# Products of the register rows over the 16 value columns of a head, and the experts' bias products on four row groups

## Chip, core and metric

The kernel is one program on one core of a Trainium2 chip. The metric is the device time of one execution in microseconds (us), lower is better; times of a kernel are medians over several executions. All data are float32. In the trace every float32 matmul of the program appears as two pairs of instructions, a weight load (PEld, LDWEIGHTS, the stationary operand) and a matmul (PE, MATMUL, the moving operand), so that four products of the program are 8 rows' worth of instructions. A float32 transpose appears as one such pair.

## What is computed

Four layers run over `x` of 8 tiles (sequences) x 512 tokens x 256 channels. Each does `x = x + s(xn) * silu(f(xn))` with `xn` the layer norm of `x`. Two places matter here. The gate branch of layer 1 is a mixture of 8 experts over all tokens:

```python
logits = xt @ Wr + br
gates = entmax_bisect(logits)                       # (tokens, 8), 25 bisection steps
gates = where(gates > 1e-9, gates, 0)
h = relu(einsum('td,edf->etf', xt, W1) + b1[:, None, :])    # F = 1024
y = einsum('etf,efd->etd', h, W2) + b2[:, None, :]
out = einsum('etd,te->td', y, gates)                # so b2 enters as gates @ b2
```

The gate branch of layer 3 is attention in which the first 5 tokens of a sequence are register rows (16 heads of 16 channels). An ordinary token sees only keys of its own set (and the registers); a register row takes the mean of two attentions, one over each set:

```python
x_pos, x_neg = masked_attn(pos), masked_attn(~pos)
reg_out = (x_pos[:, :REG] + x_neg[:, :REG]) * 0.5
tok_out = where(pos, x_pos[:, REG:], x_neg[:, REG:])
```

## The kernel before

Every layer is one block in which TensorE, VectorE (DVE), ScalarE (ACT), GpSimd (POOL) and SyncE (SP, it issues the transfers) each follow an order of instructions written out by hand; semaphores join them. PSUM banks are handed round by the classes `Jobs` (layer 1) and `Flow` (layer 3): `open` makes TensorE wait until the bank's last user has emptied it, `fill` marks the last matmul into it, `wait_filled` and `empty` are the reader's side.

**Layer 1** (function `layer1`) goes through the 8 tiles one after the other. For a tile TensorE does, in this order: the convolution's inputs `xb` (L1152) and `z` (L1157); `expert_in(0)` (L1112: for each of 8 blocks f of 128 hidden units, two products of 512 columns into one of two banks `hid`, which ACT empties with a relu, L1236); `expert_in(1)` without its last block; then, once DVE has the gates, the transposes `gt` of the gates (L1104, four tiles of 128 tokens x 8 experts into one bank of 8 x 512); the last block of `expert_in(1)`; the four bias products `b20` to `b23` (L1169: 8 experts x 128 tokens against `b2`, 8 x 256, each into a bank of its own); `expert_out(0)` (L1122: for each of 4 token tiles j, 8 products of 256 columns into one of two banks `exp_out`); `expert_in(2)`; the running sums `cum` of the state space part; and so on through expert 7. All matmuls of L1169 stand on partitions 0 to 7, so on the first of the array's four groups of 32 rows.

DVE, meanwhile: copy `gt` out (L1407), copy the four `b2` banks to `moe` (L1410), wait for its own last copy, then the convolution (L1420, L1422), four taps of 5 instructions; after tap k it adds the product of expert 0 and token tile k (`expert_sum`, L1403), for which it waits if TensorE has not filled the bank. The last tap sets `conv_ready`. ACT does the relus of experts 0 and 1, waits for `conv_ready`, and then mixes silus of the convolution (L1257, two at a time, then L1260, L1261) with relus of expert 2: two silus, relu 0, two silus, relu 1, two short silus, relu 2, and the rest. `expert_in(2)` needs bank 0 of `hid` back after its second block (relu 0), bank 1 after the third (relu 1) and bank 0 after the fourth (relu 2).

The gates of the next tile are found by DVE during expert 7 and the next tile's first products; those of the first tile have nothing before them, and TensorE stands waiting for them once.

**Layer 3's** second block (`layer3_sets`) runs 16 steps per tile. In a step TensorE does four score products and four transposed score products (L386, L393, each of 32 rows x 512 columns on one of the four row groups), the value products of the step before (L408), and a share of the work around the attention, in `last_tile`, `this_tile` and `next_tile`. The values `v_ones` hold 32 columns per head: 16 of the value, a one and zeros. In step 15 `this_tile` multiplies the transposed weights of the register rows (`reg_prob_t`, 128 x 128 for each of 4 key tiles) with all 512 columns of `v_ones` (L2872, bank `rv`). DVE waits for that bank, takes 16 of each head's 32 columns, times the inverse sum and a mask, to `reg_y` (L3093), and goes on with the next layer norm and row maxima. TensorE later sums `reg_y` over the heads (L2839).

Of the kernel before, what the change touches and what calls it, by code (L numbers as in the profile page):

```python
# [19 lines left out]
P = 128  # L20
# [940 lines left out]
def layer1(nc, b2_dram, w1_dram, w2_dram, x_all, cst, ahead, norms):  # L961
    (WZ, WX, WBC, WS, WO, CW, CB, SB, ALOG, DROW, NW, B1), width = spans(*L1_SIZES)
    with ExitStack() as ctx:
        a = Alloc(nc, ctx, "l1")
        w, b2 = ahead.w, a.sb("b2", [E, C])
        w1, w2 = a.sb("w1", [P, 2, CT, F]), a.sb("w2", [P, 2, HF, C])
        norm = ahead.norm
        xn, xn_t = norm.xn, a.sb("xn_t", [P, CT, T])
# [14 lines left out]
        half, tau_lo, width_, tau = a.sb("half", [P, TJ, E]), a.sb("tau_lo", [P, TJ]), a.sb("width_", [P, TJ]), a.sb("tau", [P, TJ])  # L983
        over, part, mass, mass_lo, step = (a.sb("over", [P, TJ, E]), a.sb("part", [P, TJ, E]), a.sb("mass", [P, TJ]),
                                           a.sb("mass_lo", [P, TJ]), a.sb("step", [P, TJ]))
        gates, gates_t = a.sb("gates", [P, TJ, E]), a.sb("gates_t", [E, T])
        hidden, moe = a.sb("hidden", [P, 2, HF, T]), a.sb("moe", [P, TJ, C])
        s = y[:, :, 0:C]

# [49 lines left out]
        @block.sync  # L1039
        def _(sp):  # L1040
            def load(e):
                sp.dma_start(w1[:, e % 2], w1_dram[e]).then_inc(w1_loaded[e % 2], 16)
                sp.dma_start(w2[:, e % 2], w2_dram[e]).then_inc(w2_loaded[e % 2], 16)

            def spread_cums(j):
                sp.dma_start(mix[:, j % 2].rearrange("p h l -> p (h l)"),
                             cum_dram[j].rearrange("h l -> (h l)").partition_broadcast(P)).then_inc(cum_loaded[j], 16)

            def stream(b, n, jobs):
                for e in range(n):  # L1050
                    nxt = (e + 2) % E
                    hid.wait_filled(sp, b, (e, HF - 1))
                    sp.dma_start(w1[:, e % 2], w1_dram[nxt]).then_inc(w1_loaded[e % 2], 16)
                    if e == 1:
                        jobs.wait_emptied(sp, b, "cum")
                        sp.dma_start(cum_dram.rearrange("j h l -> (j h) l"), cum_rows[:, :]).then_inc(cum_written, 16)
                        sp.wait_ge(cum_written, 16 * (b + 1))
                        spread_cums(0)
                        spread_cums(1)
                    if 2 <= e < TJ:  # L1060
                        jobs.wait_filled(sp, b, f"yd{e - 2}")
                        spread_cums(e)
                    exp_out.wait_filled(sp, b, (e, TJ - 1))
                    sp.dma_start(w2[:, e % 2], w2_dram[nxt]).then_inc(w2_loaded[e % 2], 16)

            sp.dma_start(b2[:, :], b2_dram).then_inc(b2_loaded, 16)
            load(0)
            load(1)
            with sp.Fori(0, B - 1) as b:
                stream(b, E, ring)  # L1070
            stream(B - 1, E - 2, last_ring)

        @block.tensor
        def _(pe):
# [23 lines left out]
            def sequence(b, is_last):  # L1098
# [60 lines left out]
                expert_in(0)  # L1159
                expert_in(1, range(HF - 1))  # L1160
                pe.wait_ge(gates_ready, b + 1)
                tiles_t("gt", lambda j: gates[:, j, :], E, 0)
                expert_in(1, [HF - 1])
                jobs.wait_emptied(pe, b, "gt")
                if b == 0:
                    pe.wait_ge(b2_loaded, 16)
                for j in range(TJ):
                    bank = jobs.open(pe, b, f"b2{j}")
                    jobs.fill(nc.tensor.matmul(bank[:, 0:C], gates_t[:, j * P:(j + 1) * P], b2[:, :], start=True, stop=True), f"b2{j}")  # L1169
                for e in range(E):  # L1170
                    if e >= 1:
                        if e + 1 < E:
# [151 lines left out]
        def _(dve):  # L1324
# [2 lines left out]
                uses.start_empty(dve)  # L1327
            dve.wait_ge(ahead.w_loaded, 16)
            V.memset(xbc[:, :, 0:TAPS - 1], 0.0)
            for f in range(FT):  # L1330
                V.tensor_scalar(wo[:, f, :], wo[:, f, :], w[:, NW][:, f:f + 1], None, ALU.mult).then_inc(prepared, 1)
            dve.wait_ge(act_prepared, 1)
# [46 lines left out]
            def sequence(b, is_last):  # L1379
# [24 lines left out]
                                                         ALU.mult, ALU.add), (e, j))  # L1404

                bank = jobs.wait_filled(dve, b, "gt")
                jobs.empty(V.tensor_copy(gates_t[:, :], bank[0:E, :]), "gt")  # L1407
                for j in range(TJ):
                    bank = jobs.wait_filled(dve, b, f"b2{j}")
                    jobs.empty(V.tensor_copy(moe[:, j, :], bank[:, 0:C]), f"b2{j}")  # L1410
# [1337 lines left out]
def layer3_sets(nc, w_dram, l3c, x_all, s_all, meanvar, rstd, set_q, set_k, cst, out_dram):  # L2748
# [6 lines left out]
    with ExitStack() as ctx:  # L2755
# [40 lines left out]
        def _(pe):  # L2796
# [60 lines left out]
            def this_tile(b, i):  # L2857
                if i == 4:
                    pe.wait_ge(reg_ready, b + 1)
                    att.wait_moved(pe, b, 3)  # L2860
                    bank = flow.open(pe, "score", ("rs", b))
                    for g in range(G):
                        ins = nc.tensor.matmul(bank[g * SLOT:(g + 1) * SLOT, :], reg_blocks[:, g, :], att.k_t[:, g, :], start=True, stop=True)  # L2863
                    flow.fill(ins, ("rs", b))
                elif i == 7:
                    flow.wait_emptied(pe, ("rs", b))
                    transposes(("rt", b), lambda j: reg_prob[:, j * P:(j + 1) * P])
                elif i == 15:
                    flow.wait_emptied(pe, ("rt", b))
                    bank = flow.open(pe, "score", ("rv", b))  # L2870
                    for j in range(TJ):
                        ins = nc.tensor.matmul(bank[:, :], reg_prob_t[:, j * P:(j + 1) * P], att.v[:, b % 2, j].rearrange("p h e -> p (h e)"),  # L2872
                                               start=j == 0, stop=j == TJ - 1)
                    flow.fill(ins, ("rv", b))

# [134 lines left out]
        def _(dve):  # L3010
# [61 lines left out]
            def this_tile(b, i):  # L3072
                if i == 2:
                    for g in range(G):
                        att.wait_moved(dve, b, g)
                    for s in range(HPG):
                        rows = slice(s * SLOT, s * SLOT + D)
                        ins = V.tensor_copy(reg_q[rows, :, :], att.q_t[rows, :, 0:REG])
                    st.link(ins)
                    for g in range(G):  # L3080
                        ins = V.tensor_tensor(reg_blocks[:, g, 0:HPG * REG].rearrange("p (s r) -> p s r", r=REG),
                                              reg_q[:, g, :].unsqueeze(1).to_broadcast([P, HPG, REG]),
                                              l3c[:, SLOT_MASK].unsqueeze(2).to_broadcast([P, HPG, REG]), ALU.mult)
                    ins.then_inc(reg_ready, 1)
                elif i == 4:
                    bank = flow.wait_filled(dve, ("rs", b))
                    V.tensor_reduce(reg_max[:, :], bank[:, :], AX, ALU.max, negate=True).then_inc(reg_max_ready, 1)
                elif i == 15:
                    flow.wait_emptied(dve, ("rs", b))
                    st.link(V.reciprocal(reg_sum[:, :], reg_sum[:, :]))  # L3090
                    bank = flow.wait_filled(dve, ("rv", b))
                    products = bank[:, :].rearrange("p (h e) -> p h e", e=att.VD)[:, :, 0:D]
                    ins = V.scalar_tensor_tensor(heads(reg_y[:, :]), products, reg_sum[:, 0:1], heads(l3c[:, HEAD_MASK]), ALU.mult, ALU.mult)  # L3093
                    flow.empty(ins, ("rv", b))
                    flow.wait_emptied(dve, ("rv", b))
                    dve.sem_inc(reg_y_ready, 1)
# [171 lines left out]
```

## Time and profile before

| | us |
|---|---|
| median of 3 runs | 4514.52 (4509.23 to 4521.08) |
| profiled execution, span from first to last instruction | 4517.0 |
| PE busy | 4370.8 (97%) |
| PEld busy | 2560.5 (57%) |
| DVE busy | 2493.9 (55%) |
| ACT busy | 1686.0 (37%) |
| POOL busy | 201.4 (4%) |
| mean granted TensorE clock | 0.983 of full speed |

The profiled execution has no time of its own beside its span; the span is 2.5 us (0.06%) above the median of the runs and within them. Times in the rows below are us from the start of the span. A busy matmul overlaps with its neighbours, so what a group costs TensorE is read from its start to the start of what follows.

### The profile page before, as it was taken

To read this page: it belongs to the slowest core of one execution; us is meant where nothing else is said; L and a number is where in the kernel's file an instruction comes from. 1 tells how busy PE (TensorE), PEld (TensorE's weight loads), DVE (VectorE), ACT (ScalarE), POOL (GpSimd) and SP (SyncE) were. 2 spreads that over 40 slices of the span, in tenths; PEclk is the share of its full clock that TensorE was granted. 3 is DMA by queue.
4 is the path that set the end of the run, shared out by engine and by line. 5 is a ranking of instruction groups with operands and counts; after the bars stand their busy time and mean duration, and the time that the engine had idled before them with its cause. 6 is when DMAs were issued, how large, how long until landed. Compare 5 with 4: busy or idle time off the path is not lost. (4 is left out here: it accounts for less than half of the span.)

```text
span 4517.0 us, 56247 instructions
## 1 busy us (share of the span) xinstructions
PE 4370.8 (97%) x19737; PEld 2560.5 (57%) x19737; DVE 2493.9 (55%) x5791; ACT 1686.0 (37%) x3239; POOL 201.4 (4%) x324
## 2 busy tenths in 40 slices
PE   7999989999999999999999999999999898999999
PEld 3444545666667566666766666566656454333333
DVE  6666653252433425243252523787899798666665
ACT  2444442232222423223232232444443322455555
POOL 0221210000000000000000000000000000000000
PEclk8999999999999999999999999999999899999999
DMA  3011112112121121212111121000000000111110
GB/s 84 16 19 32 18 45 76 61 66 84 56 82 68 71 79 56 75 66 84 73 68 66 56 94 63 9 1 1 1 1 1 20 1 16 21 20 24 26 23 21
DMA packets 51491, 196.47 MB, mean 43 GB/s; under 512 B 9720, under 2 KB 19328, under 8 KB 34184
## 3 DMA queue, kind: packets, MB, share of 16 engines
q1 hardware_dynamic: 50416, 192.84, 13.0%
q8 instruction: 160, 2.62, 0.2%
q14 instruction: 99, 0.81, 0.1%
q10 hardware_dynamic: 816, 0.20, 0.0%
HBM read 169.54 MB, written 4.33 MB: 38 GB/s over the span
## 5 line engine op out<-in xcount | busy, mean ns | idle before, releaser
L1122 PE MATMUL l_exp_out<-l_w,l_hidden 128*128 128x256 f32 x4096 | 905.3, 381 | 0.4
L1112 PE MATMUL l_hid<-l_xn_t,l_w 128*128 128x512 f32 x2048 | 891.1, 593 | 0.0
L1122 PEld LDWEIGHTS l_exp_out<-l_w,l_hidden 128*128 128x128 f32 x4096 | 774.1, 190 | 118.9 <-issue 9.0
L1236 ACT ACTIVATE l_hidden<-l_hid,l_w 128x512 f32<-128x512 f32 x512 | 351.3, 686 | 930.3 <-PE l_hid L1112 930.3
L1112 PEld LDWEIGHTS l_hid<-l_xn_t,l_w 128*128 128x128 f32 x2048 | 388.9, 190 | 466.4 <-issue 453.6
L506 DVE TENSOR_REDUCE l3f_row_max<-l3f_bank 128x1 f32<-128x512 f32 x512 | 327.7, 685 | 176.8 <-PE l3f_bank L386 176.4
L1403 DVE SCALAR_TENSOR_TENSOR l_moe<-l_exp_out,l_gates,l_moe 128x256 f32<-128x256 f32 x256 | 123.7, 483 | 450.4 <-PE l_exp_out L1122 444.8
L462 ACT ACTIVATE l3f_prob_t<-l3f_bank 128x512 f32<-128x512 f32 x512 | 277.2, 596 | 217.9 <-PE l3f_bank L393 217.9
L503 DVE CUSTOM_DVE_ANT_0 l_masked<-l_bank,l_mask 128x256 f32<-128x256 f32 (+3 forms) x512 | 226.8, 487 | 159.5 <-PE l_bank L386 158.5
L393 PE MATMUL l3f_bank<-l3f_qk_t 32*128 32x512 f32 x1024 | 303.0, 637 | 0.9 <-ACT l3f_prob_t L462 0.5
L386 PE MATMUL l3f_bank<-l3f_qk_t 32*128 32x512 f32 x1024 | 297.2, 644 | 6.6 <-DMA l3f_qk_t<-l3f_packed 6.4
L1453 DVE TENSOR_TENSOR l_y<-l_bank,l_y 128x512 f32<-128x512 f32 x32 | 22.1, 691 | 454.4 <-PE l_bank L1137 454.4
L462 ACT ACTIVATE l_prob_t<-l_bank 128x256 f32<-128x256 f32 (+3 forms) x512 | 194.6, 436 | 207.1 <-PE l_bank L393 202.7
L393 PE MATMUL l_bank<-l_qk_t 32*128 32x512 f32 (+3 forms) x1024 | 217.7, 480 | 9.0 <-ACT l_prob_t L462 8.0
L386 PE MATMUL l_bank<-l_qk_t 32*128 32x512 f32 (+3 forms) x1024 | 218.5, 495 | 6.0 <-DMA l_qk_t<-in_alibi 5.5
L386 PEld LDWEIGHTS l3f_bank<-l3f_qk_t 32*128 32x128 f32 x1024 | 83.8, 184 | 98.7 <-issue 78.5
L493 POOL TENSOR_SCALAR_AFFINE_SELECT l_prob_t<-l_prob_t 128x256 f32<-128x256 f32 x256 | 116.6, 457 | 499.9 <-ACT l_prob_t L462 499.5
L408 PE MATMUL l3f_bank<-l3f_prob_t,l3f_v_ones 128*32 128x512 f32 x1024 | 138.0, 605 | 0.0
L393 PEld LDWEIGHTS l3f_bank<-l3f_qk_t 32*128 32x128 f32 x1024 | 87.6, 183 | 78.1 <-issue 57.3
L393 PEld LDWEIGHTS l_bank<-l_qk_t 32*128 32x128 f32 x1024 | 92.1, 183 | 68.4 <-issue 44.1
L1313 POOL TENSOR_SCALAR_AFFINE_SELECT l_mix<-l_mix 128x1024 f32<-128x1024 f32 x32 | 40.8, 1275 | 1982.7 <-DMA l_mix<-l_cum 1982.7
L386 PEld LDWEIGHTS l_bank<-l_qk_t 32*128 32x128 f32 x1024 | 86.5, 188 | 75.2 <-issue 59.9
(467 smaller groups left out, 6064.8 us busy)
## 6 DMA issues: line engine op xcount, KB each, us to landing
l_w<-in_w SPq DMA_DIRECT2D x128, 1024.0 KB, 4.9
l_mix<-l_cum SPq DMA_DIRECT2D x32, 512.0 KB, 3.8
l_qk_t<-l_packed SPq DMA_DIRECT2D x128, 64.0 KB
l3f_qk_t<-l3f_packed SPq DMA_DIRECT2D x128, 64.0 KB
all_x<-in_x SPq DMA_DIRECT2D x8, 512.0 KB, 6.4
out_x<-all_x SPq DMA_DIRECT2D x7, 512.0 KB, 3.0
l_hidden<-in_fp4w SPq DMA_DIRECT2D x1, 2304.0 KB
l_qk_t<-l_max_rows SPq DMA_DIRECT2D x128, 2.0 KB
```

What stands on the lines that cost most here:

```text
L386: flow.fill(nc.tensor.matmul(bank[:, 0:keys], self.q_t[rows, g, qt * P:(qt + 1) * P], self.k_t[rows, g, 0:keys], start=True, stop=True), ( ...
L393: flow.fill(nc.tensor.matmul(bank[:, 0:T - q.start], self.k_t[rows, g, kb * P:(kb + 1) * P], self.q_t[rows, g, q], start=True, stop=True), ...
L408: ins = nc.tensor.matmul(bank[self.rows(s), q], self.v[:, b % 2, kb, g * HPG + s, :], self.prob_t[:, u % (self.LAG + 1), s, 0:T - q.start] ...
L462: flow.empty(nc.scalar.activation(self.prob_t[:, t % (self.LAG + 1), s, 0:T - q.start], bank[:, 0:T - q.start], ACT.Exp), ("t", t, s))
L493: nc.gpsimd.affine_select(block, block, [[0, 2], [1, P]], ALU.is_ge, 0.0, 0, -1).then_inc(self.selected, 1)
L503: ins = nc.vector.tensor_tensor_reduce(self.masked[:, flow.index(("s", w, s)), 0:keys], bank[:, 0:keys], mask[:, T - keys:T], 1.0, NEG, AL ...
L506: ins = nc.vector.tensor_reduce(out, bank[:, 0:keys], AX, ALU.max)
L1112: ins = nc.tensor.matmul(bank[:, :], w1[:, e % 2, c, f * P:(f + 1) * P], xn_t[:, c, :], start=c == 0, stop=c == CT - 1)
L1122: ins = nc.tensor.matmul(bank[:, 0:C], hidden[:, e % 2, f, j * P:(j + 1) * P], w2[:, e % 2, f, :], start=f == 0, stop=f == HF - 1)
L1236: hid.empty(nc.scalar.activation(hidden[:, e % 2, f, :], bank[:, :], ACT.Relu, bias=w[:, B1][:, e * HF + f:e * HF + f + 1]), (e, f))
L1313: nc.gpsimd.affine_select(mix[:, j % 2], mix[:, j % 2], [[0, SH], [1, P]], ALU.is_ge, NEG, 0, -1).then_inc(cum_masked, 1)
L1403: exp_out.empty(V.scalar_tensor_tensor(moe[:, j, :], bank[:, 0:C], gates[:, j, e:e + 1], moe[:, j, :], ALU.mult, ALU.add), (e, j))
```

## The change

Three edits. In layer 3, the products of `rv` read from `v_ones` the 16 value columns of each head alone, 256 columns in 16 runs of 16 with gaps of 16, and write 256 contiguous columns; DVE reads those. In layer 1, the gates lie in slots of 32 columns per token tile (`gates_slots`, zeroed once), so one transpose of 128 x 128 puts the gates of token tile j on partitions 32j to 32j+7, and DVE copies out 128 x 128 in place of 8 x 512. And `b2` is loaded four times, onto the same partitions, so that the four bias products stand on the four row groups. SP issues four transfers of `b2` in place of one ahead of the experts' first weights.

```diff
-        w, b2 = ahead.w, a.sb("b2", [E, C])
+        w, b2 = ahead.w, a.sb("b2", [P, C])
...
-        gates, gates_t = a.sb("gates", [P, TJ, E]), a.sb("gates_t", [E, T])
+        gates_slots, gates_t = a.sb("gates", [P, TJ, SLOT]), a.sb("gates_t", [P, P])
+        gates = gates_slots[:, :, 0:E]
...
-            sp.dma_start(b2[:, :], b2_dram).then_inc(b2_loaded, 16)
+            for j in range(TJ):
+                sp.dma_start(b2[j * SLOT:j * SLOT + E, :], b2_dram).then_inc(b2_loaded, 16)
...
                 pe.wait_ge(gates_ready, b + 1)
-                tiles_t("gt", lambda j: gates[:, j, :], E, 0)
+                bank = jobs.open(pe, b, "gt")
+                jobs.fill(nc.tensor.transpose(bank[:, 0:P], gates_slots[:, :, :].rearrange("p j e -> p (j e)"), ident), "gt")
                 expert_in(1, [HF - 1])
                 jobs.wait_emptied(pe, b, "gt")
                 if b == 0:
-                    pe.wait_ge(b2_loaded, 16)
+                    pe.wait_ge(b2_loaded, 16 * TJ)
                 for j in range(TJ):
                     bank = jobs.open(pe, b, f"b2{j}")
-                    jobs.fill(nc.tensor.matmul(bank[:, 0:C], gates_t[:, j * P:(j + 1) * P], b2[:, :], start=True, stop=True), f"b2{j}")
+                    rows = slice(j * SLOT, j * SLOT + E)
+                    jobs.fill(nc.tensor.matmul(bank[:, 0:C], gates_t[rows, :], b2[rows, :], start=True, stop=True), f"b2{j}")
...
             V.memset(xbc[:, :, 0:TAPS - 1], 0.0)
+            V.memset(gates_slots[:, :, :], 0.0)
...
-                jobs.empty(V.tensor_copy(gates_t[:, :], bank[0:E, :]), "gt")
+                jobs.empty(V.tensor_copy(gates_t[:, :], bank[:, 0:P]), "gt")
...
-                        ins = nc.tensor.matmul(bank[:, :], reg_prob_t[:, j * P:(j + 1) * P], att.v[:, b % 2, j].rearrange("p h e -> p (h e)"),
+                        ins = nc.tensor.matmul(heads(bank[:, 0:C]), reg_prob_t[:, j * P:(j + 1) * P], att.v[:, b % 2, j, :, 0:D],
                                                start=j == 0, stop=j == TJ - 1)
...
-                    products = bank[:, :].rearrange("p (h e) -> p h e", e=att.VD)[:, :, 0:D]
+                    products = heads(bank[:, 0:C])
```

## Rows read from the trace of the kernel before

**Rows 1.** Stretches: us, busy us (count) of PE, PEld, DVE, ACT, POOL, clock, DMA

```profile
1230.00:1500.00 270.00, 269.95 (x1003) 177.16 (x1002) 100.55 (x336) 80.18 (x147) 10.68 (x8) 1.00 0.20 73
...
3870.00:4500.00 630.00, 629.11 (x3862) 231.76 (x3862) 410.29 (x762) 357.42 (x677) 0.00 (x0) 1.00 0.11 22
```

**Rows 2.** Timeline, layer 3, register products: start, duration, what [idle before it <-releaser]

```profile
3950.96 3.70 PE L2872 MATMUL l3f_bank<-l3f_v_ones,l3f_reg_prob_t 128*128 128x512 f32 x8
...
3954.59 0.70 PE L393 MATMUL l3f_bank<-l3f_qk_t 32*128 32x512 f32 x2
...
3954.77 0.48 DVE L3093 SCALAR_TENSOR_TENSOR l3f_reg_y<-l3f_bank,l3f_reg_sum,l_l3c 128x256 f32<-128x256 f32 x1 [2.36 <-PE l3f_bank L2872]
```

**Rows 3.** Timeline, layer 3, eight matmuls of 256 columns, two copies back to back

```profile
3936.29 1.99 PE L2814 MATMUL l3f_bank<-l3f_w,l3f_xn_t 128*128 128x256 f32 x8
...
3938.21 0.70 PE L393 MATMUL l3f_bank<-l3f_qk_t 32*128 32x512 f32 x2
...
3938.32 0.75 DVE L3029 COPY l3f_v_ones<-l3f_bank 128x256 f32<-128x256 f32 x2 [0.66 <-PE l3f_bank L2814]
```

**Rows 4.** Timeline, layer 1, second tile, gates to the first expert sum

```profile
970.88 0.60 PE L1104 MATMUL l_bank<-all_cst,l_gates 128*8 128x128 f32 x4
...
971.31 1.88 PE L1112 MATMUL l_hid<-l_xn_t,l_w 128*128 128x512 f32 x4
971.51 0.68 DVE L1407 COPY l_gates_t<-l_bank 8x512 f32<-8x512 f32 x1 [5.71 <-PE l_bank L1104]
...
973.12 1.99 PE L1169 MATMUL l_bank<-l_b,l_gates_t 8*128 8x256 f32 x8
...
973.86 1.72 DVE L1410 COPY l_moe<-l_bank 128x256 f32<-128x256 f32 x4 [1.67 <-PE l_bank L1169]
...
975.04 14.08 PE L1122 MATMUL l_exp_out<-l_w,l_hidden 128*128 128x256 f32 x64
975.89 2.36 DVE L1420 TENSOR_SCALAR l_conv<-l_xbc,l_w 128x512 f32<-128x512 f32 x5 [0.31 <-DVE l_moe L1410]
978.80 0.48 DVE L1403 SCALAR_TENSOR_TENSOR l_moe<-l_exp_out,l_gates,l_moe 128x256 f32<-128x256 f32 x1 [0.55 <-PE l_exp_out L1122]
```

**Rows 5.** Timeline, layer 0, four products of 256 columns on four row groups

```profile
573.70 0.48 PE L386 MATMUL l_bank<-l_qk_t 32*128 32x256 f32 x2
...
574.35 0.70 PE L602 MATMUL l_bank<-l_mix_k,l_w 128*128 128x512 f32 x1
574.43 0.42 DVE L503 CUSTOM_DVE_ANT_0 l_masked<-l_bank,l_mask 128x256 f32<-128x256 f32 x1 [0.81 <-PE l_bank L386]
```

**Rows 6.** Timeline, layer 1, second tile, the products into expert 2

```profile
986.93 3.38 DVE L1422 SCALAR_TENSOR_TENSOR l_conv<-l_xbc,l_w,l_conv 128x512 f32<-128x512 f32 x5
...
988.96 13.90 PE L1112 MATMUL l_hid<-l_xn_t,l_w 128*128 128x512 f32 x32
...
990.35 1.15 ACT L1257 ACTIVATE l_conv<-l_conv 128x512 f32<-128x512 f32 x2 [16.43 <-DVE l_conv L1422]
...
992.12 0.46 PEld L1112 LDWEIGHTS l_hid<-l_xn_t,l_w 128*128 128x128 f32 x2 [0.40 <-ACT l_hidden L1236]
...
995.61 0.41 PEld L1112 LDWEIGHTS l_hid<-l_xn_t,l_w 128*128 128x128 f32 x2 [0.45 <-ACT l_hidden L1236]
```

**Rows 7.** Timeline, layer 1, first tile, before the gates are known and after

```profile
642.79 0.23 DVE L1340 TENSOR_TENSOR l_small<-l_bank,l_w 128x64 f32<-128x64 f32 x1 [3.48 <-PE l_bank L1090]
...
695.93 1.02 PE L1104 MATMUL l_bank<-all_cst,l_gates 128*8 128x128 f32 x4 [9.09 <-DVE l_gates L1371]
...
700.29 3.78 PE L1169 MATMUL l_bank<-l_b,l_gates_t 8*128 8x256 f32 x8
...
704.00 8.13 PEld L1122 LDWEIGHTS l_exp_out<-l_w,l_hidden 128*128 128x128 f32 x28 [0.65 <-issue]
```

**Rows 8.** Stretches of layer 1's first tile, columns as in Rows 1

```profile
702.00:708.00 6.00, 6.00 (x14) 4.26 (x14) 3.64 (x8) 0.00 (x0) 0.00 (x0) 0.50 0.00 0
708.00:712.00 4.00, 4.00 (x19) 3.49 (x18) 2.02 (x4) 0.00 (x0) 0.00 (x0) 0.93 0.00 0
```

## The prediction

> **What bounds the kernel now.** I read the stretches by stage first, then the waits of TensorE, then the timeline around each edited line. In the stretches the reader is to see that TensorE has no free time where the edits stand: 269.95 of 270 us in a tile of layer 1, 629.11 of 630 us in layer 3's attention, at the full clock [rows 1]. VectorE and ScalarE are busy for less than two thirds there. So time taken from TensorE comes off the end, as long as no other engine is then late. One place has TensorE idle: the first tile of layer 1, where it waits 9.09 us for the gates [rows 7].
>
> The timeline shows what a matmul costs. Eight matmuls of 512 columns (four products) take from 3950.96 to 3954.59, 3.63 us [rows 2]; eight of 256 columns take from 3936.29 to 3938.21, 1.92 us [rows 3]. The cost follows the columns of the moving operand, about 0.427 and 0.214 us each, plus 0.21 us once where the next matmuls use other row groups.
>
> **Part 1, register rows.** Per tile 3.63 us become 1.92 us: 1.71 us less. Who must keep up? VectorE waits 2.36 us for this bank today [rows 2], so it waits still after losing 1.71; everything that it does next (the product to `reg_y`, the layer norm, the maxima) hangs on the bank and moves forward with it. TensorE's steps after the bank keep their distance to VectorE. 8 tiles, 13.7 us.
>
> No row shows a moving operand in runs of 16 columns with gaps. The bounds: at the rate of contiguous columns 13.7 us are gained; if the gaps were read like columns, 0. Every product in the rows goes by its columns, whatever its operands' places, so I take 13.7.
>
> **Part 2, the gates' transpose.** Four transposes take from 970.88 to 971.31, 0.43 us, 0.11 each [rows 4]. One remains, and the load of its 128 columns in place of 8 runs under the matmul ahead of it, a 512-column one. I take 0.30 us off; the bounds are 0.32 (three of four) and 0.21 (one more 0.11 uncovered for the load that follows it). The copy behind it shrinks from 8 x 512 (0.68 us) to 128 x 128 and was hidden anyway: it begins at 971.51 and the bias products need it at 973.12 [rows 4]. VectorE had waited 5.71 us for the transposes, so the gates are ready early enough for any shift of 0.3 us.
>
> **Part 3, the bias products.** All four stand on row group 0 and take from 973.12 to 975.04, 1.92 us [rows 4]. The nearest row for four groups is layer 0's: four products of 256 columns, begun at 573.70, are over at 574.35 where the next full-height one starts, 0.65 us [rows 5]. They have 32 rows where these have 8; 1.92 us for 8-row products, the same as for 128-row ones [rows 3], says that rows do not count. So TensorE can be 1.27 us earlier at `expert_out(0)`.
>
> That is not what the tile gains. The place to look at is `expert_in(2)`, 16 us later, where TensorE gets its two `hid` banks back from ScalarE, which begins only when VectorE has finished the convolution. Its third block needs relu 0: its weight load comes at 992.12, released by ScalarE and not by the queue, and its matmul is due at 988.96 + 8 x 0.429 = 992.39; a load needs 0.11 us, so the margin is 0.16 us. The fifth block's load comes at 995.61, again released by ScalarE, with its matmul due at 995.82: margin 0.10 us [rows 6]. Today this costs nothing. If TensorE comes 1.27 us earlier, it waits, unless VectorE and ScalarE come earlier too.
>
> They do in part. (a) The first copy of a bias bank starts 0.74 us after the first bias matmul today [rows 4] and 0.73 us after in the four-group pattern [rows 5]: no change. Today four copies take 1.72 us, one bank each 0.43 us as TensorE fills them. With all banks full at once they run back to back: two such take 0.75 us where one takes 0.42 [rows 3], so four take 0.42 + 3 x 0.33 = 1.4 us; 0.3 us gained. (b) After the first tap VectorE waits 0.55 us for the first product of expert 0 [rows 4]; that product is 1.27 us earlier, so after losing 0.3 us to (a) the 0.55 go fully. From there VectorE has taps of 3.4 us and sums of 0.5 us with no waits. The convolution therefore ends 0.3 + 0.5 = 0.8 us earlier, and ScalarE, which waits 16.43 us for it [rows 6], follows at once. TensorE gains 1.27 us, ScalarE 0.8; of the 0.47 us between them the margin covers 0.10. About 0.35 us of new waiting appears in `expert_in(2)`, and part 3 is worth 0.9 us a tile. Bounds: 1.27 (nothing waits) and 0.1 (VectorE gains nothing, only the margin is used). I take 0.9, since each of (a) and (b) has its row.
>
> The Trainium skill, "TensorEngine Tiling (Array Packing)", section Performance Considerations, warns that tiling the array speeds TensorE but not the emptying of PSUM, which may then bind. The trace agrees in kind: the four copies cost VectorE about as much as before, and what binds in the end stands behind them. Were the copies alone to set the pace, part 3 would be worth (a) and the margin, 0.4 us a tile, and the sum would be 20.2 us: 4494.3.
>
> After `expert_in(2)` all later events of the tile (running sums, masks, state products) start from TensorE's own matmuls, so they shift with it.
>
> Steady tile: 0.3 + 0.9 = 1.2 us; 7 tiles, 8.4 us.
>
> **The first tile** runs after the 9.09 us wait at granted clock 0.50, 1.2 GHz, and is back at the upper level soon after 708 us [rows 8]. Its bias products take 3.71 us (700.29 to 704.00) [rows 7], its transposes twice the 0.43 us of a later tile, about 0.85. At half rate they become about 0.2 and 1.2, 3.1 us less. If the clock rises at the same moment as now, the freed 3.1 us are filled with later work at half rate, which is worth 1.6 us; if it rises as much earlier, 3.1. I take 1.6. VectorE does not bind here: TensorE is at half rate, and VectorE is busy for 3.64 of 6 us beside it [rows 8]. The gates themselves are not later: the new clearing of 128 columns stands on VectorE ahead of a wait of 3.48 us for TensorE's first products [rows 7]; uncovered it would cost less than the 0.68 us of a copy of 512 columns [rows 4], once. SP issues three more transfers ahead of the experts' first weights; TensorE has 9.09 us of waiting behind its first expert products [rows 7], which would swallow a delay of theirs.
>
> **Sum.** 13.7 + 8.4 + 1.6 = 23.7 us. Against the profiled execution's span of 4517.0 us: 4493.3. The median of the runs is 2.5 us under that span, so 4514.5 - 23.7 = 4490.8 us, 0.52% less. The three runs shown spread by 11.9 us, 0.26%, so within 0.3% (13.5 us) is about what a measurement cannot tell from no change.
>
> **Rivals.**
> - *Nothing waits.* The margin in `expert_in(2)` is wider than I read or VectorE gains more. Then 7 x 1.57 + 3.1 + 13.7 = 27.8 us: 4486.7. Against it: the weight loads already released by ScalarE [rows 6]. 0.12.
> - *The convolution keeps its time.* (a) and (b) fail, for example because copies back to back are no faster; part 3 is worth 0.1 a tile: 13.7 + 7 x 0.4 + 1.6 = 18.1 us: 4496.4. 0.10.
> - *Not side by side.* The 8-row products do not overlap across row groups, so the change doesn't do there what it says: 13.7 + 7 x 0.3 + 0.3 = 16.1 us: 4498.4. Against it: 32-row ones do [rows 5]. 0.06.
> - *The gaps cost.* The register products still take 3.63 us: only 10.0 us are gained: 4504.5. 0.08.
> - *Slower.* The strided read goes far below the contiguous rate in runs of 16. At a factor f over the contiguous 1.71 us of the matmuls, part 1 loses 13.7 x (f - 2) and outweighs the 10.0 us of layer 1 from f = 2.7; at f = 4, 27.4 - 10.0 = 17.4 us are lost: 4531.9. Only a read paying for each run anew would do it, and no row hints at one. 0.03.
>
> The Trainium skill, "SBUF — State Buffer", section Door 1: The DMA port swizzle, in a note on cachelines, says that reads within a 16-byte line run at full rate and that crossing lines costs; a run of 16 float32 values is whole lines, so by the page the gaps are free. No row here shows it.
>
> **Chances and range.** The forecast, with part 3 between 0.6 and 1.1 us a tile, has 0.61 and its own range is 4486 to 4495. The range takes in the first three rivals and the scatter of a median of a few runs, about 4 us: 4482 to 4502. It leaves out the last two and some scatter. Faster by over 0.3%: the forecast and the first three rivals, less scatter that lifts one of the latter over the bound, 0.84. Within: 0.13. Slower: 0.03.
>
> **What the trace after would show.** L2872 as eight matmuls of 128x256, 1.9 us to the next matmul; if they last 3.6 us, the gaps cost. One L1104 matmul for the gates. L1169 with matmuls started in fours within 0.03 us and L1122 0.65 us after the first. L1410 four copies in 1.4 us, no wait at the first L1403. In `expert_in(2)` two weight loads waiting for ScalarE, PE idle of 0.3 to 0.4 us in all; if it is 0, the first rival holds, if it is over 1 us, the second. Tile period of layer 1 down by 1.2 us, of layer 3 by 1.7 us. What would make me wrong altogether: a wait of TensorE in layer 3 after the register products, or a drop of the granted clock outside the first tile.

## The result, and the profile after

| | before | after |
|---|---|---|
| median of the runs, us | 4517.8 (4 runs, 4509.23 to 4521.14) | 4489.35 (4 runs, 4488.45 to 4493.77) |
| profiled execution, span, us | 4517.0 | 4492.0 |
| PE busy, us | 4370.8 | 4344.5 |
| mean granted TensorE clock | 0.983 | 0.984 |

The ratio of the times is 0.9939, with a 95% interval of 0.9925 to 0.9952: the kernel became faster by 0.6%. The forecast was 4490.8 us, 23.7 below the median of before that was known then (4514.52); the medians above differ by 28.4. The profiled execution of the kernel after is the slowest of its four: its time is 4493.77 us, 1.8 us more than its span. In the profile after, the line numbers of the two functions are some lines higher: L1165 is the gates' transpose, L1173 the bias products, L1114 and L1124 the products into and out of an expert (L1112 and L1122 before), L1415 the copies of the bias banks, L2877 the register products.

The stretches of the profile after, with the columns of [rows 1]:

```profile
1230.00:1500.00 270.00, 269.81 (x1002) 176.30 (x1001) 100.77 (x341) 80.57 (x147) 10.69 (x8) 1.00 0.19 71
...
3870.00:4475.00 605.00, 604.61 (x3819) 226.41 (x3821) 400.11 (x743) 353.80 (x672) 0.00 (x0) 1.00 0.11 22
```

TensorE is as full as before. This view cannot show a gain: the same window simply holds more work. So the comparison needs distances between the same instruction of both traces.

| stretch, us | before | after | difference |
|---|---|---|---|
| start to the gates' transpose of the first tile | 695.93 | 698.30 | +2.37 |
| from there to the transpose of the second tile | 274.95 | 271.64 | -3.31 |
| from there to the transpose of the eighth tile | 1612.96 | 1606.13 | -6.83 |
| from there to the start of layer 3's first block | 946.25 | 942.55 | -3.70 |
| layer 3's first block | 304.55 | 304.58 | +0.03 |
| layer 3's second block, to the start of its last group of products (L2831, after: L2836) | 672.73 | 659.18 | -13.55 |
| sum | 4507.37 | 4482.38 | -24.99 |

Of edited work the first row holds only the clearing of the slots and the transfers of `b2`, and it differs before they can matter: from layer 1's first matmul to the transpose it is 59.49 us before and 59.72 after, so 2.1 of the 2.37 us lie ahead of layer 1. The fourth row is mostly work of layer 2. Both are taken up below; the others answer to the parts of the sum.

**Register rows.** The timeline of the profile after, where [rows 2] stood before:

```profile
3939.51 1.99 PE L2877 MATMUL l3f_bank<-l3f_v_ones,l3f_reg_prob_t 128*128 128x256 f32 x8
3941.43 0.70 PE L393 MATMUL l3f_bank<-l3f_qk_t 32*128 32x512 f32 x2
3941.61 0.48 DVE L3098 SCALAR_TENSOR_TENSOR l3f_reg_y<-l3f_bank,l3f_reg_sum,l_l3c 128x256 f32<-128x256 f32 x1 [0.66 <-PE l3f_bank L2877]
```

From 3939.51 to the next matmul at 3941.43 it is 1.92 us, where [rows 2] have 3.63. VectorE still waits for the bank, 0.66 us in place of 2.36, and no wait of TensorE comes after it. The period of a tile falls from 80.86 to 79.15 us, by 1.71.

**Layer 1, second tile**, answering to [rows 4] and [rows 6]. The timeline of the profile after:

```profile
969.94 0.27 PE L1165 MATMUL l_bank<-all_cst,l_gates 128*128 128x128 f32 x1
...
970.05 1.88 PE L1114 MATMUL l_hid<-l_xn_t,l_w 128*128 128x512 f32 x4
...
971.86 0.71 PE L1173 MATMUL l_bank<-l_b,l_gates_t 8*128 8x256 f32 x8
...
972.50 14.08 PE L1124 MATMUL l_exp_out<-l_w,l_hidden 128*128 128x256 f32 x64
972.59 1.42 DVE L1415 COPY l_moe<-l_bank 128x256 f32<-128x256 f32 x4 [2.05 <-PE l_bank L1173]
...
974.32 2.37 DVE L1425 TENSOR_SCALAR l_conv<-l_xbc,l_w 128x512 f32<-128x512 f32 x5 [0.31 <-DVE l_moe L1415]
...
976.83 0.48 DVE L1408 SCALAR_TENSOR_TENSOR l_moe<-l_exp_out,l_gates,l_moe 128x256 f32<-128x256 f32 x1
...
986.42 14.36 PE L1114 MATMUL l_hid<-l_xn_t,l_w 128*128 128x512 f32 x32
...
988.38 1.15 ACT L1261 ACTIVATE l_conv<-l_conv 128x512 f32<-128x512 f32 x2 [15.73 <-DVE l_conv L1427]
989.44 0.67 ACT L1240 ACTIVATE l_hidden<-l_hid,l_w 128x512 f32<-128x512 f32 x1
...
990.16 0.30 PEld L1114 LDWEIGHTS l_hid<-l_xn_t,l_w 128*128 128x128 f32 x2 [0.97 <-ACT l_hidden L1240]
991.77 0.40 PEld L1114 LDWEIGHTS l_hid<-l_xn_t,l_w 128*128 128x128 f32 x2 [0.46 <-ACT l_hidden L1240]
993.64 0.30 PEld L1114 LDWEIGHTS l_hid<-l_xn_t,l_w 128*128 128x128 f32 x2 [0.62 <-ACT l_hidden L1240]
...
1000.62 0.30 PE L1181 MATMUL l_bank<-l_da,all_cst 128*128 128x32 f32 x2
```

One by one: the transpose costs 0.11 us (969.94 to 970.05) in place of 0.43. The bias products cost 0.64 us (971.86 to 972.50) in place of 1.92, so 1.28 are saved. The four copies take 1.42 us in place of 1.72. From the start of the first tap (L1425) to the first L1408 it is 2.51 us in place of 2.91, so 0.40 of the wait of 0.55 us there are gained and 0.14 stay as a gap. Then a part of the gain is lost again: `expert_in(2)` takes from 986.42 to 1000.62, 14.20 us, where before it took 13.74. A row's duration (14.36) is no measure of a stall; the start of what follows is. The releasers name the reason: three weight loads (the prediction had two) come after a relu of ScalarE and so late that TensorE stands. ScalarE is late because it cannot begin before VectorE has finished the convolution; it waits 15.73 us for it.

**First tile**, answering to [rows 7], from the timeline of the profile after:

```profile
698.30 0.47 PE L1165 MATMUL l_bank<-all_cst,l_gates 128*128 128x128 f32 x1 [9.10 <-DVE l_gates L1376]
...
702.12 1.24 PE L1173 MATMUL l_bank<-l_b,l_gates_t 8*128 8x256 f32 x8
...
703.29 16.06 PE L1124 MATMUL l_exp_out<-l_w,l_hidden 128*128 128x256 f32 x64
```

and its stretches, to be read against [rows 8] (the clock is the first number after POOL's pair):

```profile
706.00:707.00 1.00, 1.00 (x4) 0.81 (x3) 1.00 (x4) 0.00 (x0) 0.00 (x0) 0.50 0.00 0
707.00:708.00 1.00, 1.00 (x6) 0.83 (x5) 0.47 (x2) 0.00 (x0) 0.00 (x0) 0.83 0.00 0
708.00:709.00 1.00, 1.00 (x6) 0.90 (x5) 0.00 (x0) 0.00 (x0) 0.00 (x0) 1.00 0.00 0
```

The same second of these, in the profile before:

```profile
708.00:709.00 1.00, 1.00 (x5) 0.85 (x4) 0.00 (x0) 0.00 (x0) 0.00 (x0) 0.74 0.00 0
```

Before, the clock went from 1.2 to 2.4 GHz within 708 to 709, some 12.6 us after the gates' transpose at 695.93. After, it does within 707 to 708, and the transpose is at 698.30: 9.0 us. At the lower level the transposes take 0.27 us (698.30 to the next matmul at 698.57) in place of 0.81, and the bias products 1.17 (702.12 to 703.29) in place of 3.71: 3.08 us together. And the lower level ends about 3.5 us sooner after the transpose.

### The profile page after: what moved, and what is told of

Its sections match the earlier page's. It is cut to its first block and busy times, and to the rows that moved or that the text cites. A ratio compares the mean times of both kernels' runs of the same rounds, so it can differ in the third digit from the quotient of the medians.

```text
span 4492.0 us, 56203 instructions
## 1 busy us (share of the span) xinstructions
PE 4344.5 (97%) x19713; PEld 2546.9 (57%) x19713; DVE 2488.8 (55%) x5792; ACT 1686.2 (38%) x3239; POOL 202.0 (4%) x324
## 5 line engine op out<-in xcount | busy, mean ns | idle before, releaser
L1124 PE MATMUL l_exp_out<-l_w,l_hidden 128*128 128x256 f32 x4096 | 905.1, 381 | 0.4
L1114 PE MATMUL l_hid<-l_xn_t,l_w 128*128 128x512 f32 x2048 | 893.0, 594 | 0.8
L1124 PEld LDWEIGHTS l_exp_out<-l_w,l_hidden 128*128 128x128 f32 x4096 | 773.9, 190 | 118.9 <-issue 9.0
L1114 PEld LDWEIGHTS l_hid<-l_xn_t,l_w 128*128 128x128 f32 x2048 | 387.8, 190 | 472.4 <-issue 454.3
L1408 DVE SCALAR_TENSOR_TENSOR l_moe<-l_exp_out,l_gates,l_moe 128x256 f32<-128x256 f32 x256 | 123.7, 483 | 447.7 <-PE l_exp_out L1124 440.6
L493 POOL TENSOR_SCALAR_AFFINE_SELECT l_prob_t<-l_prob_t 128x256 f32<-128x256 f32 x256 | 116.6, 457 | 502.1 <-ACT l_prob_t L462 501.6
```

The lines of the kernel that those rows point to most:

```text
L493: nc.gpsimd.affine_select(block, block, [[0, 2], [1, P]], ALU.is_ge, 0.0, 0, -1).then_inc(self.selected, 1)
L1114: ins = nc.tensor.matmul(bank[:, :], w1[:, e % 2, c, f * P:(f + 1) * P], xn_t[:, c, :], start=c == 0, stop=c == CT - 1)
L1124: ins = nc.tensor.matmul(bank[:, 0:C], hidden[:, e % 2, f, j * P:(j + 1) * P], w2[:, e % 2, f, :], start=f == 0, stop=f == HF - 1)
L1408: exp_out.empty(V.scalar_tensor_tensor(moe[:, j, :], bank[:, 0:C], gates[:, j, e:e + 1], moe[:, j, :], ALU.mult, ALU.add), (e, j))
```

## The experiments

Nine kernels. Three of them were executed several times, and for them a ratio to the kernel before is given with its interval (that kernel has a median of 4515.98 us over 19 executions there). The other six were executed once each and are read by their traces.

### The register rows alone

The kernel before, with the edit of layer 3 and nothing else:

```diff
-                        ins = nc.tensor.matmul(bank[:, :], reg_prob_t[:, j * P:(j + 1) * P], att.v[:, b % 2, j].rearrange("p h e -> p (h e)"),
+                        ins = nc.tensor.matmul(heads(bank[:, 0:C]), reg_prob_t[:, j * P:(j + 1) * P], att.v[:, b % 2, j, :, 0:D],
...
-                    products = bank[:, :].rearrange("p (h e) -> p h e", e=att.VD)[:, :, 0:D]
+                    products = heads(bank[:, 0:C])
```

> The kernel before with the register rows' edit alone. My account: L2872's eight matmuls take 1.92 us to the next matmul instead of 3.63, nothing in layer 3 waits for it, 13.7 us over 8 tiles, so some 0.30% below the kernel before (ratio 0.997), and layer 1 as before (b2 products 1.92 us, expert_in(2) 13.74 us). Rival, the parts interact or a share of the 25 us between the two profiles is not of the edits: then this kernel's layer 3 stretch differs from 13.7 us less, or the sum of the two single parts' ratios misses the whole's 0.9939 by more than its interval.

Measured: 4501.01 us against 4515.98, ratio 0.9965 (0.9954 to 0.9977), which is 10 to 21 us. In the trace the products cost 1.92 us, and from the first tile's register products to the last group of products it is 542.72 us, where before had 556.41 and after has 542.87: 13.7 us, as reckoned. Layer 1 is as before, 1.92 us for its bias products and 13.74 for `expert_in(2)`.

This trace has two surprises. In the first tile of layer 1 the clock is up about 2.8 us after the transposes, though nothing of layer 1 is edited:

```profile
692.56 1.01 PE L1104 MATMUL l_bank<-all_cst,l_gates 128*8 128x128 f32 x4 [8.88 <-DVE l_gates L1371]
...
696.15 1.99 PE L1169 MATMUL l_bank<-l_b,l_gates_t 8*128 8x256 f32 x8
```

with its stretches:

```profile
694.00:696.00 2.00, 2.00 (x4) 0.64 (x2) 0.29 (x1) 0.00 (x0) 0.00 (x0) 0.67 0.00 0
696.00:698.00 2.00, 2.00 (x9) 1.40 (x8) 1.10 (x3) 0.69 (x1) 0.00 (x0) 1.00 0.04 8
```

The interval from the first tile's transposes to the second's is 270.17 us, 4.8 less than before, and no edit did it. And at the start of layer 3's second block the clock stays low for longer, so that the first register products come 6.6 us later after the block's start than in all other traces (122.92 us; 116.3 to 116.6 in the others). Here are its stretch and that of the kernel after:

```profile
3857.00:3872.00 15.00, 14.52 (x41) 7.24 (x41) 10.52 (x18) 1.55 (x2) 0.00 (x0) 0.77 0.18 29
```

```profile
3857.00:3872.00 15.00, 14.53 (x68) 6.42 (x66) 13.12 (x25) 4.92 (x8) 0.00 (x0) 1.00 0.15 24
```

In both the clock rises at another moment, each time in one profile; what moved it is not shown.

### The edits of layer 1 alone

The kernel after, with the register products as before (the diff above, turned round).

> The kernel before with the layer 1 edits alone. My account: 1.14 us less in each of tiles 2 to 8 (0.32 transposes, 1.28 bias products, 0.46 given back in expert_in(2)), about 8 us, and 1.6 to 3.3 us in the first tile depending on when the clock rises: 10 to 11 us, ratio about 0.9976. Rival, the gain behind layer 1 (the stretch from the last gates transpose to layer 3 was 3.7 us shorter between the profiles, of which the last tile explains 1.2) is caused by the edits too: then 13 us and the same 2.5 us between layer 1's end and layer 3's start again.

Measured: 4505.33 us, ratio 0.9977 (0.9968 to 0.9986), which is 6 to 14 us. The trace has layer 1 as in the kernel after: 267.67 us a tile, `expert_in(2)` 14.19 us, 271.65 from the first to the second transpose; and layer 3's end is as before, 556.49 us. The product of the two single ratios is 0.9942, the whole change's 0.9939: no sign that the parts touch each other.

The rival that was put beside this account is not settled. From the eighth tile's transpose to layer 3 it is 942.68 us here, as in the kernel after (942.55) and 3.6 less than before (946.25), of which the last tile explains 1.27. So the 2.4 us in layer 2 are there again, with no edit in layer 2. But the times are 10.65 us apart, and with 6 to 14 us they allow the 10 to 11 of the account as well as the 13 of the rival.

### The relu ahead of the silus

If `expert_in(2)` loses time because relu 0 of expert 2 stands behind two silus of the late convolution, then the relu ahead of them must give it back. Relus 0, 1 and 2 each move ahead of a pair of silus, in the kernel after:

```diff
                 for f in range(FT):
-                    nc.scalar.activation(conv[:, f, :], conv[:, f, :], ACT.Silu).then_inc(conv_act, 1)
-                    if f % 2:
+                    if f % 2 == 0:
                         relus(2, [f // 2])
+                    nc.scalar.activation(conv[:, f, :], conv[:, f, :], ACT.Silu).then_inc(conv_act, 1)
+                relus(2, [FT // 2])
...
-                        relus(e + 1, range(FT // 2 if e == 1 else 0, HF))
+                        relus(e + 1, range(FT // 2 + 1 if e == 1 else 0, HF))
```

> The changed kernel, with each of ScalarE's first three relus of expert 2 moved ahead of the two silus of the convolution that stood before it. If the 0.46 us a tile in expert_in(2) is TensorE waiting for its bank behind those silus, expert_in(2) is back at 13.74 us, the tile period falls by 0.46 us to 267.2, and the kernel is some 3.2 us (0.07%) faster than the changed one. Rival, the 0.46 us is another cost of the four row groups or of a slower start of the matmuls: then expert_in(2) stays at 14.2 us.

Measured: `expert_in(2)` takes 13.74 us again, and the period of a tile is 267.22 us, 0.46 less than after. The timeline of this kernel:

```profile
986.24 13.90 PE L1114 MATMUL l_hid<-l_xn_t,l_w 128*128 128x512 f32 x32
...
999.98 0.30 PE L1181 MATMUL l_bank<-l_da,all_cst 128*128 128x32 f32 x2
```

So the new waiting is where it was read, and without that order of ScalarE it is gone. The time is 4492.55 us, ratio 0.9946 (0.9933 to 0.9959). By the trace 3.2 us should come off the kernel after (4489.35 us, 0.9939), but the median is 3.2 us above it; the intervals of the two ratios overlap for the most part, so this gain is shown in the trace and not in the times.

### The same in the kernel before

> The kernel before with the same move of relus. My account: before the change the order cost nothing, so expert_in(2) stays at 13.74 us and the tile period at 268.8 us; only the weight loads released by ScalarE are gone. Rival, the order of the relus is worth something in itself: the tile period falls here too.

Measured: 4516.01 us, `expert_in(2)` 13.74 us and a period of 268.82 us, both to 0.01 us those of the kernel before. The stall did not exist before; it came with the edits.

### Two of the four copies on ScalarE

The kernel after, with the bias banks 2 and 3 copied by ScalarE, behind the relus of expert 1:

```diff
                 relus(1)
+                for j in (2, 3):
+                    copy_out(f"b2{j}", moe[:, j, :], C)
                 act.wait_ge(conv_ready, b + 1)
...
-                for j in range(TJ):
+                for j in range(2):
                     bank = jobs.wait_filled(dve, b, f"b2{j}")
```

> The changed kernel with two of the four copies of the bias banks on ScalarE, which is waiting then. My account: VectorE begins the convolution about 0.5 us earlier (two copies of 0.33 less, the last wait ends with ScalarE's second copy), ScalarE's silus follow, and expert_in(2) falls from 14.2 to 13.7 or 13.8 us. Rival, the 0.46 us do not come from VectorE's convolution by way of ScalarE: expert_in(2) stays at 14.2 us.

Measured: the two engines copy side by side, and from the first copy VectorE reaches the convolution in 1.33 us (972.01 to 973.34), where the kernel after takes 1.73 (972.59 to 974.32): 0.40 us earlier, where 0.5 were expected. The timeline:

```profile
972.01 0.76 DVE L1417 COPY l_moe<-l_bank 128x256 f32<-128x256 f32 x2 [2.05 <-PE l_bank L1173]
972.10 0.66 ACT L1245 ACTIVATE l_moe<-l_bank 128x256 f32<-128x256 f32 x2
973.34 2.36 DVE L1427 TENSOR_SCALAR l_conv<-l_xbc,l_w 128x512 f32<-128x512 f32 x5 [0.58 <-DVE l_moe L1417]
```

`expert_in(2)` takes 13.80 us and the period is 267.28: 0.40 to 0.41 of the 0.46 us come back, as much as VectorE is earlier. One execution took 4489.59 us.

### Two copies more on VectorE

The kernel after, with two of the bias banks copied twice, the first time to a spare buffer that nothing reads:

```diff
                     bank = jobs.wait_filled(dve, b, f"b2{j}")
+                    if j < 2:
+                        V.tensor_copy(spare[:, j, :], bank[:, 0:C])
                     jobs.empty(V.tensor_copy(moe[:, j, :], bank[:, 0:C]), f"b2{j}")
```

> The changed kernel with two more copies of 128x256 on VectorE between the bias banks and the convolution, into a tile that nobody reads. My account: the path from VectorE by ScalarE to expert_in(2) has no slack left, so each 0.33 us goes through: expert_in(2) becomes 14.2 + 0.7 = 14.9 us and the tile period grows by 0.7. Rival, it has slack: less than 0.7.

Measured: `expert_in(2)` takes 14.87 us, 0.67 more than after, and the period is 268.34, 0.65 more. The timeline shows TensorE standing 0.81 us in one piece in the middle of it; one execution took 4498.59 us:

```profile
980.75 3.60 PE L1115 MATMUL l_hid<-l_xn_t,l_w 128*128 128x512 f32 x8
985.15 10.62 PE L1115 MATMUL l_hid<-l_xn_t,l_w 128*128 128x512 f32 x24 [0.81 <-ACT l_hidden L1241]
...
995.62 0.30 PE L1182 MATMUL l_bank<-l_da,all_cst 128*128 128x32 f32 x2
```

Two copies cost VectorE about 0.67 us at 0.33 to 0.34 each, and TensorE loses 0.67. Together with the run before: in the kernel after, TensorE's time hangs on VectorE's, one to one, at this place.

### What a gap costs the moving operand

Three kernels in which the register products read 256 columns in another pattern; all three compute other products than the reference's, of the same size. In the first they are contiguous, in the second every second value, in the third every eighth (the three added lines, in this order).

```diff
-                        ins = nc.tensor.matmul(heads(bank[:, 0:C]), reg_prob_t[:, j * P:(j + 1) * P], att.v[:, b % 2, j, :, 0:D],
+                        ins = nc.tensor.matmul(bank[:, 0:C], reg_prob_t[:, j * P:(j + 1) * P], att.v[:, b % 2, j].rearrange("p h e -> p (h e)")[:, 0:C],
+                        ins = nc.tensor.matmul(bank[:, 0:C], reg_prob_t[:, j * P:(j + 1) * P], att.v[:, b % 2, j].rearrange("p h e -> p (h e)")[:, 0:2 * C:2],
+                        ins = nc.tensor.matmul(bank[:, 0:C], reg_prob_t[:, j * P:(j + 1) * P], att.v[:, b % 2].rearrange("p j h e -> p (j h e)")[:, 0:8 * C:8],
```

> The changed kernel with the register rows' products reading the first 256 columns of the values contiguously, which are 8 heads with their ones and zeros: the register rows' output is not the reference's. If gaps of 16 between runs of 16 float32 values are free, eight matmuls take 1.92 us to the next matmul as in the changed kernel. If gaps cost, less than 1.92.

> The same with every second column of 512, a step of 8 bytes; the register rows' output is not the reference's. By the account that matmuls cost their columns: 1.92 us. By the Trainium skill's "SBUF — State Buffer", section Door 1: The DMA port swizzle, note on cachelines, two accesses per 16-byte line are still enough: 1.92 us too. If only contiguous runs are free: more.

> The same with every eighth column of 2048, a step of 32 bytes; the register rows' output is not the reference's. By the account that matmuls cost their columns whatever the places: 1.92 us. By the Trainium skill's "SBUF — State Buffer", section Door 1: The DMA port swizzle, note on cachelines, every access is on a new 16-byte line and pays: clearly more than 1.92 us, 3 us or above if the rate halves.

| moving operand, 256 float32 columns | register products, us | time of one execution, us |
|---|---|---|
| runs of 16, gaps of 16 (the change) | 1.92 | 4489.35 (median) |
| contiguous | 1.92 | 4493.05 |
| every second value | 2.00 | 4495.16 |
| every eighth value | 3.85 | 4510.25 |

The timeline of the last:

```profile
3938.88 3.92 PE L2877 MATMUL l3f_bank<-l3f_v_ones,l3f_reg_prob_t 128*128 128x256 f32 x8
...
3942.73 0.70 PE L393 MATMUL l3f_bank<-l3f_qk_t 32*128 32x512 f32 x2
```

3942.73 - 3938.88 = 3.85 us. The gaps of the change cost nothing: it takes 1.92 us like the contiguous read. A step of two values costs 4%, a step of eight the double. The note on cachelines in the Trainium skill, "SBUF — State Buffer", section Door 1: The DMA port swizzle, asks for two hits in each 16-byte line for the full rate. At every second float32 a line has two hits, and yet 0.08 us are added, so there the page and the row differ a little, and the row decides. At every eighth it has one, and the 1.93 us that are added agree with a penalty. A step of four values, which has one hit in each line too, was not run; whether it is the line or the distance that costs is not shown.

## Why the prediction was right

| step | predicted, us | measured, us |
|---|---|---|
| part 1, a tile | 1.71 | 1.71 |
| part 2, a tile | 0.30 | 0.32 |
| part 3, TensorE's products, a tile | 1.27 | 1.28 |
| part 3, given back in `expert_in(2)` | 0.35 | 0.46 |
| a steady tile of layer 1 | 1.2 | 1.14 |
| first tile of layer 1 | 1.6 | 3.3 |
| sum of the edited stretches | 23.7 | 25.0 |

**Part 1.** As forecast. Both assumptions held: VectorE had more waiting (2.36 us) than the 1.71 us that it lost, and the gaps are free. *The gaps cost* is excluded by the row, and *Slower* with it; its lever exists, since a read of single values far apart costs double, but even that is short of the factor of 2.7 from which it would have decided.

**Part 2.** It came out at the upper bound, three of four transposes: the load behind the one that remains is covered.

**Part 3.** The 8-row products do stand side by side; *Not side by side* falls. The rest is the chain that was read ahead: the copies are 0.3 us faster (1.72 to 1.42), and the first expert sum comes earlier, though by 0.40 us where (b) had 0.5. So ScalarE's first silu comes 16.52 us after the start of the bias products (971.86 to 988.38), where it came 17.23 before (973.12 to 990.35): 0.71 us earlier, where the prediction had 0.8. TensorE is 1.28 earlier, 0.57 more than ScalarE; 0.46 are waited, which leaves 0.11 for the margin (the prediction had 0.10). The mechanism is right, and the 0.1 us by which the new waiting was sized too small is that of (b). So *The convolution keeps its time* falls, which had 1.2 us of new waiting, and *Nothing waits* falls too. Three runs show that a later VectorE lengthens the stall one to one, that an earlier one wins back 0.40 us, and that another order on ScalarE wins back all 0.46. The Trainium skill, "TensorEngine Tiling (Array Packing)", section PSUM Bottleneck, says that emptying PSUM may bind after tiling and that both ScalarE and VectorE should do it. The traces agree in kind: with the copies shared, 0.40 of the 0.46 us come back. What binds, though, is what stands behind the copies: were it the copies alone, part 3 would be worth the prediction's 0.4 us a tile, and 0.82 were measured.

**The first tile** is the term that was mis-sized, 3.3 us for 1.6. The prediction had chosen that the clock rises at the same moment of the span; it rose about 3.5 us earlier after the gates, so that the other bound (3.1) was the better value. This came again: in all eight profiles with the edits of layer 1 the rise comes 8.9 to 9.3 us after the gates' transpose, and from there to the second tile's transpose it is 271.6 to 271.8 us. In two of the three without them it comes after 12.6 us, and the interval is 274.9. But in the third without them, the register rows alone, it comes after 2.8 us. So something else than the edits can move it too; what does stays open, and with it whether the 1.7 us more than forecast belong to the edits.

**The stretches without edits.** The first gates' transpose starts between 692.5 and 698.5 us over the eleven profiles: at 697.5 to 698.5 in six of the seven whose kernels have all edits and at 692.5 in the seventh, at 692.6 to 695.9 in the four others. The differences arise in layer 0, in code that no edit touches; from 40 to 60 us the granted clock is 0.59 in the profile before, 0.71 in that after and 0.83 with the register rows alone. Whether the whole change has a part in this is not shown.

The -2.4 us in layer 2 (the -3.70 less the last tile's 1.27) go with the clock. The stretch of 200 us from about 58 us after layer 2's first matmul, in the profile before and with the edits of layer 1 alone, in this order:

```profile
2870.00:3070.00 200.00, 197.67 (x743) 124.95 (x742) 159.17 (x152) 90.05 (x146) 0.00 (x0) 0.98 0.00 1
2856.00:3056.00 200.00, 197.52 (x752) 125.36 (x751) 162.18 (x154) 92.38 (x150) 0.00 (x0) 1.00 0.00 1
```

They are no free scatter. Layer 2, from its first matmul to layer 3's, takes 717.7 and 717.8 us in the kernel before and in that with the relus moved in it, 716.0 with the register rows alone, and 714.7 to 715.5 in seven of the eight profiles with layer 1's edits; the eighth, with the two copies more, has 720.5. So the gain mostly comes with the edits of layer 1, though they end before layer 2 begins; by what way, and whether it holds over many executions, no run shows. The prediction had no term for it.

**Where luck had a part.** In the two profiles +2.4 us at the start and -2.4 us in layer 2 cancel; that the spans' difference of 25.0 us is that of the edited stretches is luck. So is it that the forecast time is only 1.4 us off: the time fell by 28.4 us instead of 23.7, but the three executions of before that the prediction had were also 3.3 us below the later median. Against the 19 executions of before the drop is 26.6 us. The interval on the ratio runs from 22 to 34 us; it holds the 23.7 us of the prediction, the 25.0 of the edited stretches and the 27.4 that they make with the gain in layer 2, and cannot choose between them.

## What to carry to other kernels

Time saved on a full engine is kept only as far as the engines that hand it its buffers come forward too: after each edit find the next place where the saved engine meets another, work out the margin there from the start times in the trace, and count as saved the smaller shift plus the margin. Where something then waits, look at the order of the other engine before adding buffers: here relus stood behind silus, and moving them forward won back the wait in the trace, at no cost that the trace shows. And before a difference of a few microseconds between two profiles is given to an edit, compare the stretches that the edit does not touch, over more than two profiles: what looks like scatter in one pair can come again with the edit.

## What the runs showed of the hardware

- A moving operand of float32 in runs of 16 with gaps of 16 goes at the contiguous rate (1.92 us for eight matmuls of 256 columns); with a step of 2 it takes 2.00 us, with a step of 8 3.85 us.
- Four products of 8 rows and 256 columns on four row groups take 0.64 us together, 1.92 us on one.
- After a wait of TensorE of about 9 us at the same place, the clock came back to 2.4 GHz 8.9 to 9.3 us after the gates' transpose in eight profiles, 12.6 in two and 2.8 in one. At the start of layer 3's second block one profile of eleven lost 6.6 us by a lower clock (0.77 in its stretch, 1.00 in that of the kernel after).
- Layer 2, with the same code in all eleven profiles, took 714.7 to 720.5 us, with the granted clock of a stretch at 0.98 in a slower one and 1.00 in a faster one.
